# The end of a two-sided graph product with layer normalisation: where the mean, the weights gamma and the variance are worked out

## The reference

```python
h = maximum(layernorm(x), 0)                      # x: 5120 x 64
u = par_u[0] * par_u[1] * (diag_u[:, None] * h[:2048] @ W_u) + h[:2048]
i = par_i[0] * par_i[1] * (diag_i[:, None] * h[2048:] @ W_i) + h[2048:]
e = concatenate([u, i])
g = adj @ (adj.T @ e)                             # adj: 5120 x 5120
out = (g - mean(g)) * rsqrt(var(g) + 1e-5) * ln_gamma + ln_beta + h
return x + out                                    # mean, var over the 64 of a row
```

## Time and profile before

| | |
|---|---|
| median of 3 runs | 384.83 us (384.67 to 385.56) |
| profiled execution | 384.82 us, span 383.0 us |
| granted TensorE clock | 0.991 of 2.4 GHz, mean |
| busy | TensorE 370.1 us (97%), VectorE 233.1 (61%), ScalarE 74.0 (19%), POOL 20.3 (5%) |
| HBM | 127.36 MB read, 1.31 MB written, 336 GB/s over the span |

### The profile page before, as it was taken

The page is one execution under the profiler, slowest core; times in us unless marked ns, Lnnn a source line. Parts: engine busy times, 40 slices in busy tenths (PEclk is TensorE's granted clock), DMA queues, the critical chain, the costliest instruction groups (busy, mean ns, idle before and its releaser), DMA issues.

```text
span 383.0 us, 9909 instructions
## 1 busy us (share of the span) xinstructions
PE 370.1 (97%) x4436; PEld 194.2 (51%) x4436; DVE 233.1 (61%) x205; ACT 74.0 (19%) x213; POOL 20.3 (5%) x28
## 2 busy tenths in 40 slices
PE   6989999999999999999999999999999999999991
PEld 4656455554536454554545364545545453645451
DVE  5887994664729292746647292927466472929057
ACT  5852121202020201202020202012020202020132
POOL 2039000000000000000000000000000000000013
PEclk8999999999999999999999999999999999999998
DMA  8999999999999889798979797897979797930003
GB/s 316 419 420 417 420 420 420 423 421 419 422 362 427 314 358 369 302 424 299 428 303 427 303 428 298 362 368 305 426 303 424 298 429 299 426 120 2 2 2 137
DMA packets 19022, 128.88 MB, mean 336 GB/s; under 512 B 2112, under 2 KB 2496, under 8 KB 3648
## 3 DMA queue, kind: packets, MB, share of 16 engines
q1 hardware_dynamic: 18720, 128.28, 82.5%
q10 hardware_dynamic: 288, 0.39, 0.3%
HBM read 127.36 MB, written 1.31 MB: 336 GB/s over the span
## 4 chain that ended last, share of the span: by engine, by line
PE 87%; DMA 7%; DVE 3%; SPq 2%; issue 0%; ACT 0%
PE t_acc L554 41%; PE h_acc L583 37%; PE h_acc L567 9%; DMA cols<-adj_cols 7%; SPq L191 1%; DVE scaled L508 1%; DVE var L383 1%; DVE scaled L504 1%; SPq L188 0%; PE t_acc L611 0%; DVE xs L511 0%; DVE rstd L391 0%; ACT squares L354 0%; SPq L199 0%
## 5 line engine op out<-in xcount | busy, mean ns | idle before, releaser
L420 DVE STREAM_TRANSPOSE strips<-natural 128x2048 f32<-128x2048 f32 x80 | 177.9, 2281 | 120.0 <-PE h_acc L583 120.0
L554 PE MATMUL t_acc<-natural,e 128*64 128x256 f32 x1600 | 178.2, 381 | 1.2 <-DMA natural<-adj_rows 1.2
L554 PEld LDWEIGHTS t_acc<-natural,e 128*64 128x64 f32 x1600 | 113.7, 137 | 70.6 <-issue 15.9
L583 PE MATMUL h_acc<-strips,centred 32*64 32x512 f32 x2560 | 142.2, 590 | 0.0
L583 PEld LDWEIGHTS h_acc<-strips,centred 32*64 32x64 f32 x2560 | 54.6, 132 | 85.9 <-issue 85.9
L305 ACT COPY t_high<-t_acc 64x256 f32<-64x256 f32 x20 | 7.4, 369 | 242.4 <-PE t_acc L554 242.4
L567 PE MATMUL h_acc<-cols,centred 128*64 128x512 f32 x160 | 37.9, 594 | 0.2 <-DMA cols<-adj_cols 0.2
L312 ACT COPY centred<-centred 32x384 f32<-32x384 f32 (+2 forms) x60 | 24.2, 403 | 39.2 <-DVE centred L431 38.7
L313 ACT COPY centred<-centred 32x128 f32<-32x128 f32 (+2 forms) x60 | 23.8, 397 | 0.0
L263 POOL TENSOR_TENSOR xs<-scaled,xs 128x512 f32<-128x512 f32 x4 | 5.1, 1267 | 335.3 <-DVE scaled L508 335.3
L567 PEld LDWEIGHTS h_acc<-cols,centred 128*64 128x64 f32 x160 | 11.2, 137 | 15.5 <-issue 12.2
(11 more groups left out here) (39 smaller groups left out, 57.6 us busy)
## 6 DMA issues: line engine op xcount, KB each, us to landing
natural<-adj_rows SPq DMA_DIRECT2D x100, 1024.0 KB, 12.6
cols<-adj_cols SPq DMA_DIRECT2D x20, 1024.0 KB, 4.9
out<-xs SPq DMA_DIRECT2D x5, 256.0 KB, 2.0
xs<-x SPq DMA_DIRECT2D x3, 256.0 KB, 8.4
xs<-x ACTq DMA_DIRECT2D x1, 256.0 KB, 3.8
smalls<-small SPq DMA_DIRECT2D x1, 214.0 KB, 3.6
xs<-x ACTq DMA_DIRECT2D x1, 128.0 KB, 2.9
xs<-x SPq DMA_DIRECT2D x1, 128.0 KB, 2.7
```

What stands on the lines that cost most here:

```text
L420: nc.vector.transpose(strips[:, a, :, m].rearrange("p c t i -> p t c i"), natural[:, a, m].rearrange("p t (c j) -> p t c j", j=Q)).then_in ...
L554: last = nc.tensor.matmul(t_acc[D * s:D * (s + 1), a, 0:WIDE], e[:, GT * m + 2 * k + s, :], natural[:, a, m, HALF * s + k], start=(m == 0 ...
L583: last = nc.tensor.matmul(h_acc[D * s:D * (s + 1), q], t[part, a, b, u, :], rows, start=(isinstance(g, int) and g == 0 and b == 0 and u == 0),
```

## The change

Subtracting the mean of each row from g = adj @ t is the same as subtracting it from t, since adj acts on rows and the mean is over features. So:

- `keep_t` gets two more VectorE operations for each panel: `t_total`, the sum over the 64 features of each of its 32 x 8 rows, and t less 1/64 of that.
- At the end VectorE multiplies each copy out of PSUM by gamma, which is one number per partition in the turned layout. It now makes all four copies of the strips groups and the copy of the loaded one.
- ScalarE makes squares from PSUM at the same places, into `h_squares`. The sum of squares over features is a matmul of the squares (as weights) with `ones`, a 128 x 2 matrix with ones for one half of the partitions in each column: `out_var`, 8 matmuls for two groups, into `v_acc` or a free bank.
- `out_turn` becomes a plain PE transpose against `ident`. One root and one reciprocal serve two groups, and one multiplication from PSUM gives `scaled`.
- VectorE adds the residual for groups 2 and 4, POOL for 0, 1 and 3. The store of group 3 is issued by ScalarE.
- `centre` goes; gamma in `smalls` is one column instead of 64.

```diff
@@ keep_t
-                last.then_inc(s_t_part, 1)
+                last.then_inc(s_t_turned, 1)
+                rows = t[0:Q, a].rearrange("p b u d -> p (b u) d")
+                dve.wait_ge(s_t_turned, g + 1)
+                nc.vector.tensor_reduce(t_total[:], rows, AX.X, ALU.add).then_inc(s_t_total, 1)
+                dve.wait_ge(s_t_total, g + 1)
+                nc.vector.scalar_tensor_tensor(rows, t_total[:].unsqueeze(2).to_broadcast([Q, STRIPS, D]), -1.0 / D,
+                                               rows, ALU.mult, ALU.add).then_inc(s_t_part, 1)
@@ SP
-            for m in range(GROUPS):
-                if m < LOADED:
+            for m in (0, 1, 2, 4):
+                if m < 2:
                     sp.wait_ge(s_o_added, m + 1)
                 else:
-                    sp.wait_ge(s_o_done, 1)
+                    sp.wait_ge(s_o_done, m // 2)
                 sp.dma_start(out[:, rows_of(m), :], xs[:, rows_of(m), :]).then_inc(s_out, 16)
@@ POOL
-            for m in range(LOADED):
+            for n, m in enumerate((0, 1, 3)):
                 pool.wait_ge(s_o_scaled, m + 1)
@@ ScalarE
-            for half in range(2):
-                nc.scalar.copy(*strips_across(half, 0)).then_inc(s_o_low, 1)
-            square_out(0)
-            square_out(1)
+            for n, (half, q) in enumerate(((0, 2), (0, 0), (1, 0), (1, 2))):
+                if n % 2:
+                    act.wait_ge(s_o_copied, n)
+                nc.scalar.activation(*strips_across(h_squares, half, q), ACT.Square).then_inc(s_o_squares, 1)
+            out_deviation(0)
             act.wait_ge(s_loaded_done, PANELS)
-            nc.scalar.copy(across[:, 0], h_acc[:, LOADED]).then_inc(s_o_loaded, 1)
-            for m in range(2, GROUPS):
-                square_out(m)
+            nc.scalar.activation(across[:, 1], h_acc[:, LOADED], ACT.Square).then_inc(s_o_squares, 1)
+            out_deviation(2)
+            out_deviation(4)
+            act.wait_ge(s_o_added, 3)
+            act.dma_start(out[:, rows_of(3), :], xs[:, rows_of(3), :]).then_inc(s_out, 16)
@@ VectorE
+            def out_scale(m):
+                if m % 2 == 0:
+                    dve.wait_ge(s_o_std, m // 2 + 1)
+                    nc.vector.reciprocal(out_rstd[:, tiles_of(m)], out_std[:, tiles_of(m)]).then_inc(s_o_rstd, 1)
+                    dve.wait_ge(s_o_rstd, m // 2 + 1)
+                dve.wait_ge(s_o_turned, m + 1)
...
+                nc.vector.tensor_tensor(scaled[:, m % 2], out_bank(m).rearrange("p (k d) -> p k d", d=D),
+                                        by_tile(out_rstd[:, rows_of(m)]), ALU.mult).then_inc(s_o_scaled, 1)
...
+            for n, (half, q) in enumerate(((0, 0), (0, 2), (1, 2), (1, 0))):
+                if n % 2:
+                    dve.wait_ge(s_o_squares, n)
+                nc.vector.tensor_scalar(*strips_across(h_across, half, q), gamma_s, None,
+                                        ALU.mult).then_inc(s_o_copied, 1)
+            out_scale(0)
+            out_scale(1)
+            dve.wait_ge(s_o_squares, 5)
+            nc.vector.tensor_scalar(across[:, 0], h_acc[:, LOADED], gamma_s, None, ALU.mult).then_inc(s_o_copied, 1)
+            out_scale(2)
             dve.wait_ge(s_res, GROUPS)
+            out_add(2)
+            out_scale(3)
+            out_scale(4)
+            out_add(4)
@@ TensorE
+                for j in range(m, min(m + 2, GROUPS)):
+                    for k in range(HALF):
+                        at = GT * (j - m) + 2 * k
+                        last = nc.tensor.matmul(out_vars(m)[:, at:at + 2], across_of(h_squares, 1, j, k), ones[:],
+                                                start=True, stop=True)
+                last.then_inc(s_o_var, 1)
...
+                    last = nc.tensor.transpose(out_bank(m)[:, P * k:P * (k + 1)], across_of(h_across, 0, m, k),
+                                               ident[:])
...
+            out_var(0)
             out_turn(0)
             out_turn(1)
             second_loaded(LAST, 1, LAST // 2)
-            for m in range(2, GROUPS):
-                out_turn(m)
+            out_var(2)
+            out_turn(2)
+            out_turn(3)
+            out_var(4)
+            out_turn(4)
```

More of the change, by code:

```diff
@@ L63, in gnn_layer @@
         par = smalls[:, TILES:TILES + 4].rearrange("p (n v) -> p n v", n=2)
-        gamma_s = smalls[:, GAMMA:GAMMA + D]
-        beta_s = smalls[:, GAMMA + D:GAMMA + 2 * D]
-        wdiag = smalls[:, GAMMA + 2 * D:SMALL].rearrange("p (n c) -> p n c", n=2)
+        gamma_s = smalls[:, GAMMA:GAMMA + 1]
+        beta_s = smalls[:, GAMMA + 1:GAMMA + 1 + D]
+        wdiag = smalls[:, GAMMA + 1 + D:SMALL].rearrange("p (n c) -> p n c", n=2)
         eps = sb("eps", [P, 1])
@@ L121, in gnn_layer @@
         s_strips_last = sem("s_strips_last")
[L122 to L126, removed]
+        s_o_copied = sem("s_o_copied")
+        s_o_squares = sem("s_o_squares")
+        s_o_var = sem("s_o_var")
+        s_o_std = sem("s_o_std")
+        s_o_rstd = sem("s_o_rstd")
+        s_o_turned = sem("s_o_turned")
         s_o_scaled = sem("s_o_scaled")
@@ L252, in _ @@
                                         ALU.add).then_inc(s_res, 1)
-            pool.wait_ge(s_zero, 2)
+            pool.wait_ge(s_ones_zero, 1)
             pool.wait_ge(s_res, GROUPS)
             for d in range(2):
[L256 to L260, removed]
-            for m in range(LOADED):
+                nc.gpsimd.memset(ones[D * d:D * (d + 1), d:d + 1], 1.0).then_inc(s_ones, 1)
+            for n, m in enumerate((0, 1, 3)):
                 pool.wait_ge(s_o_scaled, m + 1)
@@ L495, in _ @@
             step(LAST, LAST % 2, LAST // 2)
-            dve.wait_ge(s_strips_last, 1)
[L497 to L508, removed]
@@ new lines, in out_add @@
+            def out_add(m):
+                dve.wait_ge(s_o_scaled, m + 1)
+                nc.vector.tensor_tensor(xs[:, rows_of(m), :], scaled[:, m % 2], xs[:, rows_of(m), :],
+                                        ALU.add).then_inc(s_o_done, 1)
+            dve.wait_ge(s_strips_last, 1)
+            dve.wait_ge(s_small, 16)
+            for n, (half, q) in enumerate(((0, 0), (0, 2), (1, 2), (1, 0))):
[3 more added lines that the diff above has]
+                                        ALU.mult).then_inc(s_o_copied, 1)
@@ L595, in step, with across_of, out_var @@
                 second_strips(g - 1, 1 - a).then_inc(s_strips_done, 1)
+            def across_of(buffer, spare, m, k):
+                if m == LOADED:
+                    return across[:, spare, P * k:P * (k + 1)]
+                return buffer[:, m, k].rearrange("p q i -> p (q i)")
+            def out_var(m):
+                if m == 0:
+                    pe.wait_ge(s_ones, 2)
+                    pe.wait_ge(s_o_squares, 2)
+                elif m == 2:
+                    pe.wait_ge(s_o_squares, 4)
+                    pe.wait_ge(s_o_copied, 4)
+                else:
+                    pe.wait_ge(s_o_squares, 5)
+                    pe.wait_ge(s_o_std, 1)
+                for j in range(m, min(m + 2, GROUPS)):
[4 more added lines that the diff above has]
+                last.then_inc(s_o_var, 1)
             def out_turn(m):
                 if m == 0:
-                    pe.wait_ge(s_centre, 1)
                     pe.wait_ge(s_t_sum, PANELS)
+                    pe.wait_ge(s_o_copied, 2)
                 if m == LOADED:
[L603 to L607, removed]
+                    pe.wait_ge(s_o_copied, 5)
                 for k in range(HALF):
[L609 to L612, removed]
+                    last = nc.tensor.transpose(out_bank(m)[:, P * k:P * (k + 1)], across_of(h_across, 0, m, k),
+                                               ident[:])
+                last.then_inc(s_o_turned, 1)
             pe.wait_ge(s_idle, 1)
@@ L675 @@
         for d in range(2):
-            at = GAMMA + 2 * D + P * n + D * d
+            at = GAMMA + 1 + D + P * n + D * d
             small[D * d:D * (d + 1), at:at + D] = np.asarray(w)
-    small[:, GAMMA:GAMMA + D] = np.asarray(L0_gnn_ln_gamma)
-    small[:, GAMMA + D:GAMMA + 2 * D] = np.asarray(L0_gnn_ln_beta)
+    small[:, GAMMA] = np.tile(np.asarray(L0_gnn_ln_gamma), 2)
+    small[:, GAMMA + 1:GAMMA + 1 + D] = np.asarray(L0_gnn_ln_beta)
     arrays = {
```

44 lines of the change are left out of this document (27 added, 17 removed).

## The result

| | before | changed |
|---|---|---|
| median of 20 runs | 384.72 us (384.26 to 386.04) | 383.93 us (383.6 to 385.2) |
| profiled execution, span | 384.82, 383.0 us | 383.69, 381.9 us |

The ratio of the changed kernel to the one before is 0.9978, 95% interval 0.9971 to 0.9985: faster by 0.8 us, and inside the 0.3% that the prediction took as its bound. The two profiled executions differ by 1.13 us, more than the medians do (0.79); what is known of the reason is seen under experiments.

A forecast was written before the change was run, and what follows sets the result against it. TensorE was taken as the bound until 366.04, then rounds of four VectorE operations. From 384.82, +0.4 at panel 0, -2.0 in the tail and +0.4 for stores gave 383.6, leaned down to 383.5 us; range 381.9 to 384.8.

The forecast's parts named there:

- Middle and last panels cost nothing: After panel 0, the new VectorE work fits in waits of about 7 us, and the last panel is early by 1.6 us.
- Panel 0 costs 0.4: In the first panel, `keep_t` delays the strips, so TensorE starts 0.40 us late; bounds 0 and 0.5.
- since strips now decide, it gives nothing: At the start, shorter `smalls` brings the loads behind it forward by under 0.1 us, without gain for panel 0.
- TensorE's chain in the tail: After the last strips, variances at 0.11 us a record, transposes and loaded product hold TensorE's chain until 374.46.
- the rival of cheap small matmuls: In the tail's variances, a two-column record takes 0.058 us, giving 381.8; chance 0.1.
- the slow one: In the tail, load and small matmul don't overlap, 0.21 us a record: +3.2, giving 386.7; chance 0.06.
- The other rule: For the tail's variances, matmuls of 1 to 64 columns start about 60 cycles apart: 1.0 instead of 1.78 us each.
- VectorE's end at 378.64: In the tail, VectorE's last addition ends at 378.64 instead of 380.63, a gain of 2.0 us.
- POOL adds group 3 beside it: In the tail, POOL adds group 3 from 377.1 to 378.36 while VectorE works on group 4.
- The stores cost 0.4: At the end, the last two stores overlap and the second lands later: +0.4 us, bounds 0 and 0.5.
- likeliest case: For the whole kernel, the forecast itself, within 383.2 to 384.0 us; chance 0.5.
- The clock: Rival: a tail clock fall at about 374.5 gives 384.7, no change; at about 376 it costs nothing; chance 0.12.

The follow-up runs named there:

- tail_alone: Changed kernel with the centring taken out of `keep_t` and put nowhere else, so the mean stays in; 383.23 us, ratio 0.9966 to the kernel before.
- var_twice_wide: Changed kernel with each small matmul of `out_var` issued twice and moving 64 columns of `ones` instead of 2; 388.93 us in one execution.
- pool_late: Changed kernel with POOL's addition of group 3 made to wait for VectorE's addition of group 4; 385.09 us in one execution.
- pool_two: Changed kernel with group 2 added by POOL and group 3 by VectorE, after its scales; 383.37 us, ratio 0.9973 to the kernel before.
- pool_waits: Changed kernel with POOL's beta additions held back until `keep_t(0, 0)` is done; 383.61 us, ratio 0.9972 to the kernel before.
- var_twice: Changed kernel with each small matmul of `out_var` issued twice, same result; 393.25 us in one execution.

## Why the prediction was right, point by point

- **Middle and last panels cost nothing.** Right: 120.0 us of waiting became 93.5, and no wait for t or strips shows after panel 0.
- **Panel 0 costs 0.4.** Right as a mechanism and, alone, as a size: 0.43 between tail_alone and the changed kernel. Two things were missed beside it. The words on the shorter `smalls`, "since strips now decide, it gives nothing", were wrong: in the changed kernel the addition into `t_sum` began at 30.75 instead of 30.96, so `first`, `keep_t` and the strips behind it came earlier too, by 0.27 in all in tail_alone; the net is +0.16. That the shorter transfer does this is likely and not isolated. And the term has a spread of its own, from POOL's additions: the second operation of `keep_t(0, 0)` took 0.68 to 1.07, and 1.65 in var_twice_wide.
- **TensorE's chain in the tail.** Predicted from 366.04: variance 0 complete at 369.79, loaded part from 370.64, variance 2 complete at 374.46. Measured, from the starts of the roots less their 0.03 and less the 0.16 of the start: 369.79, 370.65, 374.47. The record of 0.11 for two moving columns held (1.95 for sixteen), and the rival of cheap small matmuls, 381.8, and the slow one, 386.7, are both refuted by that row. The rule of the Trainium skill ("TensorE: Matmul & The Clock Gate", LDWEIGHTS) on loads as long as their columns stands with it. The other rule that the prediction took from that page would have made 1.0 of these sixteen records, and they took 1.95: here, where each matmul has its own load, it doesn't give the time.
- **VectorE's end at 378.64.** With 0.16 added 378.80, measured 379.23. This is the term that was off: the step "POOL adds group 3 beside it" took the two for independent. The addition 4 took 1.02 instead of 0.69, because it reads both inputs from SBUF and had to wait for POOL; pool_late and pool_two show it. The other 0.1 is reciprocals of sixteen columns at 0.25 instead of 0.19, and a wait ahead of addition 2.
- **The stores cost 0.4.** From VectorE's end to the end of the span it was 2.40 and is 2.62: 0.2. The two stores were issued 0.54 us apart (378.71 and 379.25) instead of the 0.26 of the prediction, so they overlapped less, and the later one landed 2.2 after its issue instead of 2.4. That the distance is the reason fits the kernel before (1.40 apart, 2.0) and pool_two (0.61 apart, 2.1); it wasn't tested by itself.
- **Sum.** +0.16 - 1.56 + 0.22 = -1.18, and the spans differ by 1.2. Predicted was +0.4 - 2.0 + 0.4 = -1.2. That the sums agree is luck: the start cost 0.24 less and the stores 0.18 less than said, and the tail gained 0.44 less. The median gained only 0.8. Of the missing 0.34, 0.10 is that the profiled execution of before lay above its median; the rest is most likely that in part of the changed kernel's executions panel 0 is later, as it was by 0.31 in the second profile. pool_waits fits that and doesn't settle it. The size, 383.9, lies in the likeliest case's own range, and of the two sides of its bound the one that had the smaller chance came (0.36 against 0.58 in all): no more than 0.3%.
- **The clock.** It fell in the changed kernel too, inside the last group:

```profile
372.90:376.20 3.30, 3.30 (x32) 3.30 (x32) 1.85 (x4) 0.76 (x2) 0.94 (x1) 1.00 0.42 159
376.30:379.60 3.30, 0.74 (x5) 0.34 (x4) 2.86 (x5) 0.27 (x1) 1.26 (x1) 0.53 0.22 84
```

As the prediction had it, this fall costs nothing: VectorE takes up group 4 at 377.26, behind its own work. But the moment differs between executions. In the second profile of the changed kernel the clock was still 1.00 from 376.30 to 379.60, and in pool_waits, whose tail is the same code, it fell before 375.8 and VectorE idled 0.42 us. So "a fall at about 376 costs nothing" holds with only some tenths to spare. And var_twice shows that this rival deserved more than 0.12, since one more batch of small matmuls brings the fall ahead of work that is on the path. What the Trainium skill says of transposes ("TensorE: Matmul & The Clock Gate", PE-mode transpose) no run here tests by itself: in var_twice_wide the transposes were the same as in var_twice, and the clock didn't fall.

## What to carry to other kernels

Before an operation is moved beside another engine's, ask what both read: two additions, one on VectorE with both inputs in SBUF and one on POOL, don't run side by side. Here VectorE lost 0.25 to 0.97 us by it, and POOL 0.47. Sums that are moved to TensorE pay per weight load: sixteen records with loads of 128 columns took 1.95 with 2 columns moving and 2.05 with 128. Matmuls with few moving columns can cost the clock for what comes behind them (0.50 in var_twice); 64 columns instead of 2 cost nothing there (3.63 us for 32 records more, 3.6 expected). Work that is hidden in the steady state has to be checked in the first round by itself, where the list of instructions is another and slack was 1 us, not 7.

## What the runs showed of the hardware

- **POOL and VectorE exclude each other** when VectorE's operation has two SBUF inputs: in the changed kernel it ended 0.55 us after POOL's addition did (POOL until 377.42 + 1.26 = 378.68, VectorE until 379.23), and it took 0.68 to 0.69 without it. With one input in PSUM it wasn't held: the scale at 377.48 took 0.69 during the same POOL addition. pool_late shows it by taking the POOL addition away, pool_two by putting it earlier. The Trainium skill ("SBUF — State Buffer", SBUF: two separate sides) describes this as an exclusive lock on a shared pair of ports, which goes to whoever starts first and blocks the other; the trace agrees in both directions (POOL 1555 ns instead of 1086 where VectorE was first).
- **The granted clock fell to 0.50 while TensorE's record showed it fully busy** (4.00 of 4.00 us from 370 to 374 in var_twice), with 128 x 128 loads and 2 moving columns; with 64 columns it stayed at 1.00 (var_twice_wide). Each is one execution.
- A POOL addition of the same shape took 1086 ns in the changed kernel where it had taken 1273 in the kernel before, in the lines that add beta. Beta starts 63 columns earlier in `smalls` there. Whether that is the cause wasn't tried.
